# Last batch's projection and scores as three passes over 12-bit parts in the rounded float32 type

## What is computed

```python
def _L0_xattn_ref(teacher_logits, teacher_features, Wq, bq, Wk, bk):
    query = jnp.einsum('bnc,dc->bnd', teacher_features, Wq) + bq      # projection
    key = jnp.einsum('bnc,dc->bnd', teacher_features, Wk) + bk        # projection
    energy = jnp.einsum('bnd,bmd->bnm', query, key)                   # scores
    attention = jax.nn.softmax(energy, axis=-1)
    return jnp.einsum('bln,bmn->blm', teacher_logits, attention)

def _L0_ffn_ref(x, w1, b1, w2, b2):
    w1q, w2q = _bit_quant(w1), _bit_quant(w2)                         # -1, 0 or 1 each
    h = jax.nn.gelu(jnp.einsum('bsd,fd->bsf', x, w1q) + b1, approximate=False)
    return jnp.einsum('bsf,df->bsd', h, w2q) + b2

x = x + _L0_xattn_ref(_layernorm(x), ctx_1024, Wq, bq, Wk, bk)
x = x + _L0_ffn_ref(_layernorm(x), w1, b1, w2, b2)
```

## Time and profile before

| | |
|---|---|
| median of 3 runs | 312.23 us (311.51 to 312.27) |
| the profiled execution's own time | 312.49 us |
| its span, first to last instruction | 310.7 us |
| TensorE busy | 303.9 us of the span |
| VectorE, ScalarE, GpSimd busy | 153.7, 143.9 and 109.2 us |
| share of the chain that ended last | TensorE 96%, transfers 2%, VectorE 1% |

### The profile page before, as it was taken

The page is one execution under the profiler, slowest core; times in us unless marked ns, Lnnn a source line. Parts: engine busy times, 40 slices in busy tenths (PEclk is TensorE's granted clock), DMA queues, the critical chain, the costliest instruction groups (busy, mean ns, idle before and its releaser), DMA issues.

```text
span 310.7 us, 3674 instructions
## 1 busy us (share of the span) xinstructions
PE 303.9 (98%) x1401; PEld 144.2 (46%) x1401; DVE 153.7 (49%) x295; ACT 143.9 (46%) x253; POOL 109.2 (35%) x111
## 2 busy tenths in 40 slices
PE   6799999999999999999999999999999999999996
PEld 3366544444444444444444444444444444444455
DVE  0888896764598853755308342445433003442101
ACT  2179998577723506542654604545440017762000
POOL 0276339999979960000903620000650000000000
PEclk9999999999999999999999999999999999999999
DMA  7899999674653992000032854000034100000011
GB/s 174 237 381 408 361 277 205 131 135 103 121 104 63 155 228 105 2 0 0 0 70 54 166 103 154 0 0 0 2 69 115 56 34 0 0 2 0 34 49 54
DMA packets 66706, 32.24 MB, mean 104 GB/s; under 512 B 59504, under 2 KB 60032, under 8 KB 66176
## 3 DMA queue, kind: packets, MB, share of 16 engines
q1 hardware_dynamic: 66368, 31.73, 40.4%
q10 hardware_dynamic: 320, 0.27, 0.4%
HBM read 15.21 MB, written 4.19 MB: 62 GB/s over the span
## 4 chain that ended last, share of the span: by engine, by line
PE 96%; DMA 2%; DVE 1%; SPq 0%; ACT 0%; issue 0%
PE ps_t L511 36%; PE ps_e L536 24%; PE ps_e L494 13%; PE ps_e L525 9%; PE ps_e L443 5%; PE ps_e L435 2%; PE ps_e L543 2%; PE ps_t L435 2%; DMA ctx_sb<-in_ctx 2%; PE ps_t L467 1%; PE ps_e L454 1%; PE ps_t L454 1%; SPq L247 0%; DVE ctxT L764 0%; ACT qkT L644 0%; DVE x_sb L1055 0%
## 5 line engine op out<-in xcount | busy, mean ns | idle before, releaser
L511 PE MATMUL ps_t<-x2T,w1T 128*128 128x512 f16 x512 | 112.1, 379 | 0.0
L706 ACT ACTIVATE ps_t<-ps_t,b_col 128x512 f32<-128x512 f32 x64 | 42.5, 665 | 96.6 <-PE ps_t L511 96.6
L511 PEld LDWEIGHTS ps_t<-x2T,w1T 128*128 128x128 f16 x512 | 50.1, 98 | 60.7 <-issue 0.6
L900 DVE SCALAR_TENSOR_TENSOR gT_lo<-ps_t,h_scale,gT_hi 128x512 f16<-128x512 f32 x64 | 45.1, 746 | 66.2 <-ACT gT_hi L711 66.2
L536 PE MATMUL ps_e<-w_raw,gT_hi 128*128 128x512 f16 x176 | 66.7, 379 | 0.0
L536 PE MATMUL ps_e<-w_raw,gT_lo 128*128 128x512 f16 x176 | 66.7, 379 | 0.0
L349 POOL TENSOR_TENSOR rstd<-var_eps,minus_half 128x4 f32<-128x4 f32 (+1 forms) x9 | 8.5, 947 | 99.7 <-DVE neg_mean L813 99.7
L711 ACT ACTIVATE gT_hi<-ps_t,h_scale 128x512 f16<-128x512 f32 x64 | 40.3, 684 | 0.0
L906 DVE SCALAR_TENSOR_TENSOR x_sb<-ps_e,h_unscale,x_sb 128x512 f32<-128x512 f32 x15 | 11.0, 748 | 57.9 <-PE ps_e L536 54.6
L536 PEld LDWEIGHTS ps_e<-w_raw,gT_lo 128*128 128x128 f16 x176 | 17.2, 98 | 21.4 <-issue 1.0
L536 PEld LDWEIGHTS ps_e<-w_raw,gT_hi 128*128 128x128 f16 x176 | 17.2, 98 | 21.1 <-issue 0.7
(11 more groups left out here) (86 smaller groups left out, 290.9 us busy)
## 6 DMA issues: line engine op xcount, KB each, us to landing
w_raw<-in_L_ffn_w SPq DMA_DIRECT2D x8, 1024.0 KB, 14.7
x_sb<-in_x SPq DMA_DIRECT2D x4, 1024.0 KB, 7.5
out<-x_sb SPq DMA_DIRECT2D x15, 256.0 KB, 2.6
ctx_sb<-in_ctx SPq DMA_DIRECT2D x16, 128.0 KB, 3.2
b_sb<-in_L_ffn_b SPq DMA_DIRECT2D x1, 256.0 KB, 7.2
w_raw<-w_raw SPq DMA_TRANSPOSE x16, 3.8
out<-x_sb SPq DMA_DIRECT2D x2, 128.0 KB, 1.7
x2n<-in_L_xattn_Wq ACTq DMA_DIRECT2D x1, 128.0 KB, 3.0
```

Source lines behind the costliest of these rows:

```text
L511: mm = nc.tensor.matmul(ps_t[t][:], w1T[:, k, j], x2T[:, b % 2, v, :, j], start=(v == 0 and j == 0), stop=(v == 1 and j == ND - 1))
L706: nc.scalar.activation(ps_t[t][:], ps_t[t][:], ACT.Gelu, scale=1.0 / LN_SCALE, bias=b1_col[:, k:k + 1]).then_inc(gelu_done, 1)
L900: nc.vector.scalar_tensor_tensor(out=gT_lo[:, k], in0=ps_t[t][:], scalar=h_scale[:, 0:1], in1=gT_hi[:, k], op0=ALU.mult, op1=ALU.subtract) ...
```

## The change

Only batch 3 is touched. Its projection and its scores no longer run as float32 matmuls. Each float32 operand is cut into an upper part (the low 12 bits set to zero by a bitwise AND on VectorE) and a lower part (operand minus upper part). Both are stored in `float32r`, the rounded float32 type. Each product is then the sum of three matmuls of that type: upper by upper, upper by lower, lower by upper. So the 4 float32 matmuls of the projection become 12 of the rounded type, and so do the 4 of the scores.

The parts are made by new instructions: `cut_projection` on VectorE (two ANDs), `split_W` and `split_ctx` on GpSimd (a copy of the upper part into the rounded type, and a subtraction, each), then for the scores `split_qk` on VectorE (an AND and a subtraction) and `upper_qk` on GpSimd (a copy). The parts lie in two new tiles, `W_parts` and `parts`; the second holds first the context's parts and then those of `qkT`. The cuts stand in the free part of `w2_raw`, so `turn_xn(3)` on SyncE's queue gets three more waits.

```diff
+F32R = mybir.dt.float32r
+UPPER_BITS = -(1 << 12)
...
+        W_parts = sb("W_parts", [P, 2, 2, NC, H], F32R)
+        parts = sb("parts", [P, 2, NC * L], F32R)
...
+        ctx_cut = w2_flat[:, ST:ST + NC * L]
+        W_cut = w2_flat[:, ST + NC * L:ST + NC * L + 2 * NC * H]
+        qk_cut = w2_flat[:, ST:ST + 2 * L]
...
             def turn_xn(b):
                 if b > EARLY:
                     sp.wait_ge(attn_ready, NT * b)
+                    sp.wait_ge(qk_ready, 2 * B)
+                    sp.wait_ge(qk_upper_done, 1)
+                    sp.wait_ge(qk_lower_done, 1)
...
+            def split_W():
+                pool.wait_ge(W_cut_done, 1)
+                flat = W_parts[:].rearrange("p v s k h -> p v (s k h)")
+                nc.gpsimd.tensor_scalar(flat[:, 0], W_cut, 1.0, None, ALU.mult).then_inc(W_parts_done, 1)
+                nc.gpsimd.tensor_tensor(flat[:, 1], WT[:].rearrange("p s k h -> p (s k h)"), W_cut,
+                                        ALU.subtract).then_inc(W_parts_done, 1)
+
+            def split_ctx():
+                pool.wait_ge(ctx_cut_done, 1)
+                flat = ctx_parts.rearrange("p v k l -> p v (k l)")
+                nc.gpsimd.tensor_scalar(flat[:, 0], ctx_cut, 1.0, None, ALU.mult).then_inc(ctx_parts_done, 1)
+                nc.gpsimd.tensor_tensor(flat[:, 1], ctxT[:].rearrange("p k l -> p (k l)"), ctx_cut,
+                                        ALU.subtract).then_inc(ctx_parts_done, 1)
+
+            def upper_qk():
+                pool.wait_ge(qk_cut_done, 1)
+                nc.gpsimd.tensor_scalar(qk_parts[:, 0].rearrange("p s l -> p (s l)"), qk_cut, 1.0, None,
+                                        ALU.mult).then_inc(qk_upper_done, 1)
...
             add_b2(1)
+            split_W()
+            split_ctx()
             layernorm2(2)
+            upper_qk()
             layernorm(3)
...
+            PARTS = ((0, 0), (0, 1), (1, 0))
+
+            def project_by_parts(free):
+                pe.wait_ge(W_parts_done, 2)
+                pe.wait_ge(ctx_parts_done, 2)
+                for s in range(2):
+                    free(s)
+                    for n, (u, v) in enumerate(PARTS):
+                        for k in range(NC):
+                            mm = nc.tensor.matmul(qk_bank(LAST, s)[:], W_parts[:, u, s, k], ctx_parts[:, v, k],
+                                                  start=(n == 0 and k == 0), stop=(n == 2 and k == NC - 1))
+                    mm.then_inc(qk_ready, 1)
+
+            def scores_by_parts(tiles, free):
+                pe.wait_ge(qk_upper_done, 1)
+                pe.wait_ge(qk_lower_done, 1)
+                for t in tiles:
+                    free(t)
+                    for n, (u, v) in enumerate(PARTS):
+                        mm = nc.tensor.matmul(scores_bank(LAST, t)[:], qk_parts[:, u, 0, t * P:(t + 1) * P],
+                                              qk_parts[:, v, 1], start=(n == 0), stop=(n == 2))
+                    mm.then_inc(scores_ready, 1)
...
-                    project(3, lambda s: pe.wait_ge(x2_done, NT * 2 + s + 3))
+                    project_by_parts(lambda s: pe.wait_ge(x2_done, NT * 2 + s + 3))
                     output(b, 0)
-                    scores(3, (0, 1), scores_free(3))
+                    scores_by_parts((0, 1), scores_free(3))
                     output(b, 1)
-                    scores(3, (2, 3), scores_free(3))
+                    scores_by_parts((2, 3), scores_free(3))
...
+            def cut(out_t, in_t, done):
+                nc.vector.tensor_scalar(out_t.bitcast(I32), in_t.bitcast(I32), UPPER_BITS, None,
+                                        ALU.bitwise_and).then_inc(done, 1)
+
+            def cut_projection():
+                cut(W_cut, WT[:].rearrange("p s k h -> p (s k h)"), W_cut_done)
+                cut(ctx_cut, ctxT[:].rearrange("p k l -> p (k l)"), ctx_cut_done)
+
+            def split_qk():
+                dve.wait_ge(qkT_done, 2 * B)
+                flat = qkT[:].rearrange("p s l -> p (s l)")
+                cut(qk_cut, flat, qk_cut_done)
+                dve.wait_ge(qk_cut_done, 1)
+                nc.vector.tensor_tensor(qk_parts[:, 1].rearrange("p s l -> p (s l)"), flat, qk_cut,
+                                        ALU.subtract).then_inc(qk_lower_done, 1)
...
             moments2(2, 3)
+            cut_projection()
             aggregate2(2)
             low_gelus(1, range(12, 16))
 
+            split_qk()
             result(1, 0)
...
-    nc = bacc.Bacc("TRN2", target_bir_lowering=False, num_devices=1)
+    nc = bacc.Bacc("TRN2", target_bir_lowering=False, num_devices=1, dynamic_dma_scratch_size=4096)
```

More of the change, by code:

```diff
@@ L135, in xattn_ffn @@
                   w2_flat.bitcast(F16)[:, 2 * ST:4 * ST]]
+        ctx_parts = parts[:].rearrange("p v (k l) -> p v k l", k=NC)
+        qk_parts = parts[:].rearrange("p v (s l) -> p v s l", s=2)
+        ctx_cut = w2_flat[:, ST:ST + NC * L]
+        W_cut = w2_flat[:, ST + NC * L:ST + NC * L + 2 * NC * H]
+        qk_cut = w2_flat[:, ST:ST + 2 * L]
         def turned_half(b, n):
@@ L163, in xattn_ffn @@
         rstd2_done, x2n_done = sem("rstd2_done"), sem("x2n_done")
+        W_parts_done, ctx_parts_done, qk_upper_done = sem("W_parts_done"), sem("ctx_parts_done"), sem("qk_upper_done")
         scaled, rounded = sem("scaled"), sem("rounded")
@@ L182, in xattn_ffn @@
         xn0_read = sem("xn0_read")
+        W_cut_done, ctx_cut_done, qk_cut_done = sem("W_cut_done"), sem("ctx_cut_done"), sem("qk_cut_done")
+        qk_lower_done = sem("qk_lower_done")
         ctxT_ready, b1_col_done, b1_abs_done = sem("ctxT_ready"), sem("b1_col_done"), sem("b1_abs_done")
```

## The result

The changed kernel took 315.43 us in the median of 4 runs (314.52 to 316.70), the kernel before 312.25. The ratio is 1.011, 95% interval 1.0077 to 1.0143: slower by 1.1%, where 311.6 us was forecast. The profiled execution took 314.52 us with a span of 312.7 us, 2.0 us more than before.

What follows compares the result with a forecast made beforehand. TensorE was taken to bound the kernel: a saving of 1.69 us less a stall of 1.03 gave a net gain of 0.66, from 312.23 to 311.57 us in the median. The range was 310.8 to 312.9 us.

Steps and rivals of the forecast that it cites:

- What bounds the kernel: Whole kernel: TensorE, busy 303.9 of 310.7 us, waits for nothing around the change.
- TensorE's saving: Batch 3's projection and scores: 24 rounded-type matmuls at 0.216 us, 5.18 us in place of 6.87, saving 1.69 us.
- The place of the new wait: Ahead of batch 3's projection: TensorE waits 0.76 us for GpSimd's last subtraction.
- the absence of a wait elsewhere: Scores, later GpSimd work and attend(3), whose transposes have slack 8.6 us: all else late costs 0 us.
- the slack of 2.4: Before batch 3's scores: parts ready near 160.7 us, scores due at 163.1, so no wait; rival of a wait, chance 0.02.
- the sum of the new wait: Ahead of batch 3's projection: cuts and four GpSimd operations from 147.03 to 153.32 us, TensorE free at 152.56.
- W's upper part, 128x512 with one source: GpSimd's copy ahead of the projection: 0.75 us plus 0.23 beside other engines, giving 0.98 us.
- the context's upper part, 128x1024, one source: 1.11: GpSimd's copy ahead of the projection: 1.11 us, the fastest time of a 1024-wide one-source operation.
- the context's lower part: GpSimd's two-source subtraction of 128x1024 ahead of the projection: 2.26 us, at most 2.54.
- refilling: Batch 3's projection behind the wait: first load and fill show, 0.27 us more, making the stall 1.03 us.
- The rival of unhidden weight loads: Rounded-type matmuls on TensorE: 190 ns loads not hidden, 0.406 us each, kernel 3.90 us slower at 316.1; chance 0.10.
- GpSimd is slowed through all four steps: GpSimd ahead of the projection: slowed 1.78 times by VectorE, stall 5.0 us, loss 3.3, kernel 315.5 us; chance 0.05.

Runs made afterwards that it cites:

- e1: The changed kernel with twelve more GpSimd copies in idle time, six forms at 512 and 1024 elements, results unused; one run, 316.21 us.
- e2: The changed kernel with its three GpSimd upper-part copies as x 1.0 x 1.0 in place of x 1.0 alone; median 311.62 us, ratio to before 0.9974.
- e7: The changed kernel with the projection's parts made earlier, its ANDs behind batch 2's second moments, cuts in their own space; median 310.72 us, ratio to before 0.9958.
- e12: The changed kernel again, unaltered, beside the kernel before; median 316.23 us of 6 runs, ratio 1.0135.
- e8: The kernel before, float32, with batch 3's projection also waiting for batch 3's fourth xn tile, TensorE idle meanwhile; median 317.88 us, ratio 1.0162.
- e9: The kernel before, float32, with batch 3's projection also waiting for batch 3's first xn tile, a shorter gap; median 313.78 us, ratio 1.0041.
- e5: The changed kernel with each projection matmul cut into two of 256 columns, 24 in place of 12; one run, 317.12 us.
- e6: The changed kernel with all parts made on VectorE by copy and subtraction, the projection's early, no GpSimd operations; median 310.49 us, ratio to before 0.9955.

## Why the prediction was wrong

**What bounds the kernel** was right: TensorE, back to back, so the outcome is TensorE's saving less its new idle time. The place of the new wait, its releaser and the absence of a wait elsewhere were right too: `attend(3)` had its transposes with the same slack, and the scores' parts were in time. That last was partly luck: their copy was priced at 1.98 us and took 3.81, and 1.1 us of the slack of 2.4 was left.

**The step that failed** is in the sum of the new wait: "W's upper part, 128x512 with one source", taken as 0.98 us, and "the context's upper part, 128x1024, one source: 1.11". They took 1.86 and 2.76, 2.53 us more for the two. The rows I priced them by were all of operations with two arithmetic steps; the new ones have one, with the second absent. e1 shows that the form accounts for this (1.49 - 0.62 and 2.77 - 1.04, together 2.60 us), and e2 that the gap comes out as forecast without it: 0.61 us against 0.76. W's copy then takes the 0.98 us forecast, by luck: 0.62 for the form and 0.36 beside VectorE's cut, where I had 0.75 and 0.23. e2's time can't settle more. By its trace the gain is 1.36 - 0.61 - 0.26 = 0.49 us, where I had 0.66, and the interval of its ratio spans 0.2 to 1.4 us. The row was of the same engine, width and type, but not of the same form.

The other terms of that chain: cut of W 0.41 (0.48), W's lower part 1.26 (1.27), the context's lower part 2.33 (2.26), refilling 0.26 (0.27). For the context's lower part, the estimate from the Trainium skill (GPSIMD Engine Reference, Elementwise, side-by-side cycle accounting) was 2.35 us, and the trace agrees with it at 2.33.

**TensorE's saving** was mis-sized a little: 24 matmuls took 5.51 us without a wait (e7), not 5.18, a pace of 0.228 to 0.232 in place of 0.216. The gain is 1.36 and not 1.69 us. The rival of unhidden weight loads stood on the wrong ground: halving the columns halved the time.

**A cost I didn't name**: the granted clock behind the gap. It isn't in the first profiled run, and is 1.60 us in the traced run of e12. With that run's cost for the median of the six, 1.36 - (3.21 + 0.26) - 1.60 = -3.7 us, against 316.23 - 312.24 = 4.0 measured. The Trainium skill (TensorE: Matmul & The Clock Gate, Why this matters for your kernels) warns against idle gaps between bursts of matmuls. The runs agree for e8's gap of 3.6 us, and e9's of 1.3 us had no such cost. I had put the idle time at 0.76 us, 1.03 with refilling, so this followed from the first error: the stall came out at 3.47 us, three times as long, and in e12 at 5.07 with the clock's 1.60, five times as dear.

The rival "GpSimd is slowed through all four steps" gave the right side and nearly the right size (315.5) by the wrong mechanism: the subtractions weren't slowed at all (1.26 and 2.33 us), and what W's copy had on top beside VectorE was 0.37 us.

## What to carry to other kernels

Price a new instruction by a row of the same form, not only of the same engine, width and type; where no row has that form, the upper bound must be wider, or the form avoided. Work that is taken off a saturated engine pays only if what prepares it is early: the same preparation cost 3.2 us of idle TensorE behind batch 2's last moments and nothing 12 us earlier. Count a stall on TensorE at more than its length once it is as long as the 3.2 to 3.6 us here, since the clock may fall behind it; at 1.3 us it cost its length and the refilling alone.

## What was not expected of the hardware

- GpSimd's tensor-scalar with one operation took 1.49 us at 128x512 and 2.77 at 128x1024, with two operations 0.62 and 1.04, and a plain copy into the rounded type 1.04 at 1024; for the tensor-scalar forms the type of the output (float32 or rounded) made no difference.
- A matmul of the rounded float32 type takes 0.229 us at 512 columns and 0.119 at 256, and that of 512 is 6% over float16's 0.216.
- After TensorE had been idle for 3.2 to 3.6 us, the granted clock was 0.68 to 0.83 of full in the 5 to 10 us behind in three of five traces (e5, e8, e12). The mean clock of the run was low in 5 of 6 of e8, 6 of 6 of e12 and 2 of the first 4 of the changed kernel; that it fell behind the gap in those without a trace is inferred. The kernel before had a clock of 0.995 in one of 50 timed runs and 0.999 or more in the others.
- e6 makes both parts by a copy into the rounded type and a subtraction, with no AND; the copies took as long as the ANDs (0.41 us at 128x512, 0.69 at 128x1024). What bits the copy leaves was not read out.
